# Attention and mixture of experts in one kernel: a new order of VectorE's work at the start of a round, two PSUM banks for the last attention outputs, and a second query tile scaled by GpSimd

## What is computed

```python
x = x + attention(x, mask, null_kv=cond_64)      # 16 x 256 x 256, 16 heads of 64
x = x + moe(x, cond_64)                          # 8 experts, top 2, and 2 shared ones

def attention(x):
    xn = ln(x) * g_norm
    q = l2norm(heads(xn @ Wq)) * q_scale         # per head
    k, v = split(xn @ Wkv)                       # one key and value head for all
    k = l2norm(concat(null_k, k)) * k_scale
    sim = q @ k.T * 8 + relative_bias + null_bias, causal and masked
    return ln(softmax(sim) @ concat(null_v, v) @ Wout) * g_out

def moe(x):
    w = top2(softmax((x @ wt.T + cond @ wg.T) / 2)), normalised
    y = sum(w[e] * (leaky(x @ w_gate[e]) * (x @ w_up[e])) @ w_down[e])
    return y + leaky(x @ sw_gate) * (x @ sw_up) @ sw_down
```

## Time and profile before

| | before |
|---|---|
| median of 3 runs | 1118.29 us (1117.87 to 1120.53) |
| the profiled execution | 1119.15 us, of it a span of 1117.4 us |
| PE busy | 1018.4 us (91%) |
| PEld busy | 827.5 us |
| DVE busy | 746.6 us (67%) |
| ACT busy | 534.5 us |
| POOL busy | 446.8 us |

### The profile page before, as it was taken

One profiled execution on the slowest core, in us unless ns is written; L12 is line 12 of the kernel. 1 busy time (PEld: TensorE's weight loads), 2 busy tenths in 40 slices (PEclk: granted clock), 3 DMA queues, 4 the chain that ended last, 5 costly groups with the idle time before them and its releaser, 6 DMA issues.

```text
span 1117.4 us, 22423 instructions
## 1 busy us (share of the span) xinstructions
PE 1018.4 (91%) x7244; PEld 827.5 (74%) x7244; DVE 746.6 (67%) x2515; ACT 534.5 (48%) x1579; POOL 446.8 (40%) x422
## 2 busy tenths in 40 slices
PE   2377899999989999999999999999999999999898
PEld 1266587777878787777878787787877778787777
DVE  7768858775587747765587756876487755866443
ACT  3048725663356614665256634565156543566110
POOL 2254514553435515453245424355054433355112
PEclk9588999999999999999999999999999999999999
DMA  5064411321123211311123111321113201231032
GB/s 207 19 180 156 157 39 57 106 86 41 58 77 104 67 40 58 122 62 45 60 76 115 57 58 41 105 77 67 58 58 105 83 23 43 91 105 67 20 121 106
DMA packets 40938, 89.88 MB, mean 80 GB/s; under 512 B 4128, under 2 KB 18976, under 8 KB 40304
## 3 DMA queue, kind: packets, MB, share of 16 engines
q1 hardware_dynamic: 40816, 88.29, 23.8%
HBM read 78.67 MB, written 11.70 MB: 81 GB/s over the span
## 4 chain that ended last, share of the span: by engine, by line
PE 70%; DVE 17%; issue 7%; ACT 3%; POOL 1%; SPq 1%; DMA 0%; DVEq 0%; ACTq 0%; POOLq 0%
PE psY L1479 13%; PE psO L1406 6%; PE psS L1376 6%; PE psG L65 4%; PE psG L63 4%; PE psG L64 4%; PE psT L1387 4%; PE psS L1371 3%; PE psO L1409 2%; PE psS L63 2%; PE psT L63 2%; PE psS L65 2%; PE psT L64 2%; PE psS L64 2%; PE psT L65 2%
## 5 line engine op out<-in xcount | busy, mean ns | idle before, releaser
L557 POOL TENSOR_TENSOR work<-work,rden 128x514 f32<-128x514 f32 x128 | 134.2, 1048 | 332.6 <-DVE rden L1039 332.0
L1479 PE MATMUL psY<-Wd,H 128*128 128x256 f32 x640 | 171.6, 397 | 0.0
L683 ACT ACTIVATE work<-work,low 128x257 f32<-128x257 f32 x256 | 128.3, 503 | 74.6 <-DVE low L1057 74.4
L63 PE MATMUL psG<-x1T_hi,Wgu 128*128 128x512 f32 x280 | 130.2, 465 | 7.5 <-DVE H L1157 5.6
L1479 PEld LDWEIGHTS psY<-Wd,H 128*128 128x128 f32 x640 | 111.7, 189 | 28.0 <-issue 14.4
L1057 DVE CUSTOM_DVE_ANT_0 work<-psS,bias,null_s 128x256 f32<-128x256 f32 x256 | 113.0, 478 | 23.0 <-PE psS L1376 22.5
L1147 DVE SCALAR_TENSOR_TENSOR leaky<-leaky 128x512 f32<-128x512 f32 x80 | 56.2, 703 | 98.4 <-ACT leaky L721 98.4
L65 PE MATMUL psG<-x1T_lo,Wgu 128*128 128x512 f32 x280 | 110.4, 394 | 0.0
L546 POOL TENSOR_TENSOR rq<-qss,neghalf 128x16 f32<-128x16 f32 x32 | 96.3, 3012 | 33.6 <-DVE qss L1033 33.6
L64 PE MATMUL psG<-x1T_hi,Wgu 128*128 128x512 f32 x280 | 109.4, 391 | 0.0
L675 ACT ACTIVATE qT_hi<-psO 128x256 fp32r<-128x256 f32 x128 | 49.0, 383 | 117.4 <-PE psO L1409 115.9
(11 more groups left out here) (236 smaller groups left out, 2584.7 us busy)
## 6 DMA issues: line engine op xcount, KB each, us to landing
Wgu<-wexp SPq DMA_DIRECT2D x80, 512.0 KB, 3.3
Wb<-wscr SPq DMA_DIRECT2D x64, 256.0 KB, 3.4
wexp<-Wgu SPq DMA_DIRECT2D x10, 512.0 KB, 2.9
xin<-in_x SPq DMA_DIRECT2D x8, 512.0 KB, 3.7
xres<-in_x SPq DMA_DIRECT2D x8, 512.0 KB, 4.5
out<-work SPq DMA_DIRECT2D x8, 512.0 KB, 2.9
H<-in_wgu SPq DMA_DIRECT2D x10, 256.0 KB, 4.0
bscr<-bscr SPq DMA_DIRECT2D x1, 2048.0 KB, 12.7
```

The lines of the kernel that those rows point to most:

```text
L63: te.matmul(dst, a_hi, b_hi, start=start, stop=False)
L557: pool.tensor_tensor(T1[sl][:, hs, :], T1[sl][:, hs, :], rden[sl][:, 1, hs].unsqueeze(2) .to_broadcast([P, 2, N + 1]), ALU.mult)
L683: act.activation(T1[sl][:, h, :], T1[sl][:, h, :], ACT.Exp, scale=-1.0, bias=low[sl][:, 1, h:h + 1], accum_out=den[sl][:, 1, h:h + 1])
L1479: mm = te.matmul(psY[:, t // 2, (t % 2) * D:(t % 2 + 1) * D], H[:, k % H_RING, t * P:(t + 1) * P], Wd[:, ORDER[k], :], start=(k == 0 and t ...
```

## The change

It does five things.

1. `scale_q` of tile 2 goes from VectorE to GpSimd, where it stands between the third and the fourth `rq`.
2. VectorE's `scale_q` of tile 3 moves behind the scores of step 0.
3. `null_parts` is one pair of operations on all four tiles ahead of step 0, behind all four `rq`; the pair at step 3 is gone.
4. On VectorE `sum_q(1)` goes ahead of `router_logits`, `router_shift` behind the remainder of the keys, and `hidden(1)` ahead of the second `turned_q`. On ScalarE the exponential of the router goes behind the square of tile 2.
5. `value` of steps 12 and 14 goes to psG, and 13 and 15 stay in psO. From step 12 on a value waits for the output before the last one, and for all `hidden` of the round. TensorE's wait for `pn_done`, the last read of the null column, moves ahead of `turn_x`.

```diff
-POOL_TILES = 1
+POOL_SCALED = (0, 2)
+DVE_SCALED = (1, 3)
+LAST_VALUES = 12
...
+        def value_bank(n):
+            return psG if n >= LAST_VALUES and n % 2 == 0 else psO
...
                     pool.tensor_tensor(rq[:, t, :], qss[:, t, :], neghalf[:], ALU.pow).then_inc(rq_done.sem, 1)
-                    if t < POOL_TILES:
+                    if t in POOL_SCALED:
                         scale_q(pool, r, t, qn_pool)
...
+                sum_q(r, 1)
                 if moe is not None:
                     router_logits(moe)
-                sum_q(r, 1)
-                if moe is not None:
-                    router_shift(moe)
...
                 for n in range(4):
                     turned_q(r, n)
+                    if n == 0 and moe is not None:
+                        hidden(moe, 1)
                     if n == 1 and moe is not None:
-                        hidden(moe, 1)
                         router_weights(moe)
-                scale_q(dve, r, 2, qn_done)
                 if moe is not None:
                     leak(moe, 2)
                     hidden(moe, 2)
-                scale_q(dve, r, 3, qn_done)
-                ch = vchain["null"]
-                ch.start(r)
-                null_parts(r, ch, 0)
+                null_parts(r)
...
                         scores(r, n // STEPS, n % STEPS)
+                    if n == 0:
+                        scale_q(dve, r, 3, qn_done)
...
+                need(dve, rq_done, r, TILES)
+                ch.link(dve, dve.tensor_tensor(null_s[:], kvs[:, :, 2 * DH:], rq[:], ALU.mult))
...
+                need(te, pn_done, r, GROUPS)
                 if following is not None:
                     turn_x(following)
                 need(te, o_done, r, ALL)
-                need(te, pn_done, r, GROUPS)
...
-                need(te, o_done, r, n)
+                if n < LAST_VALUES:
+                    need(te, o_done, r, n)
+                else:
+                    need(te, o_done, r, n - 1)
+                    if moe is not None:
+                        need(te, h_done, moe, BLOCKS)
+                bank = value_bank(n)
```

More of the change, by code:

```diff
@@ L316, in attention_moe @@
         qss_done = events("qss_done", TILES)
[L317 removed]
+        qn_done = events("qn_done", len(DVE_SCALED))
         qT_v = events("qT_v", 2 * TILES)
@@ L333, in attention_moe @@
         vchain = {n: Chain(events("v_" + n, k)) for n, k in
-                  (("ln1", 2), ("knorm", 3), ("null", 4), ("ln2", 2 * TILES), ("x1", TILES), ("router", 14))}
+                  (("ln1", 2), ("knorm", 3), ("null", 2), ("ln2", 2 * TILES), ("x1", TILES), ("router", 14))}
         xnT_a = events("xnT_a", 1)
@@ L352, in attention_moe @@
         rq_done = events("rq_done", TILES)
-        qn_pool = events("qn_pool", POOL_TILES)
+        qn_pool = events("qn_pool", len(POOL_SCALED))
         norm_done = events("norm_done", ALL)
@@ L625, in attention @@
                     act.activation(sq, src, ACT.Square).then_inc(sq_done.sem, 1)
+                    if t == 2 and moe is not None:
+                        softmax(moe)
                     if t == 1 and moe is not None:
@@ L674, in head_out @@
                 need(act, pv_ps, r, n + 1)
-                act.activation(qT[0][:, STEPS * (g % 2) + s, (g // 2) * N:(g // 2 + 1) * N], psO[:, 0:N],
+                act.activation(qT[0][:, STEPS * (g % 2) + s, (g // 2) * N:(g // 2 + 1) * N], value_bank(n)[:, 0:N],
                                ACT.Copy).then_inc(o_lead.sem, 1)
@@ L924, in attention @@
                 if moe is not None:
+                    router_shift(moe)
                     leak(moe, 0)
@@ L1021, in turned_q, with null_parts @@
                                   qT[0][cols].bitcast(F32), ALU.subtract).then_inc(qT_v.sem, 1)
-            def null_parts(r, ch, bb):
-                ts = slice(2 * bb, 2 * bb + 2)
-                ch.link(dve, dve.tensor_tensor(null_s[:, ts, :], kvs[:, ts, 2 * DH:], rq[:, ts, :], ALU.mult))
-                ch.link(dve, dve.tensor_tensor(null_s[:, ts, :], null_s[:, ts, :], null_bias[:].unsqueeze(1)
-                                               .to_broadcast([P, 2, HEADS]), ALU.add))
+            def null_parts(r):
+                ch = vchain["null"]
+                ch.start(r)
+                need(dve, rq_done, r, TILES)
+                ch.link(dve, dve.tensor_tensor(null_s[:], kvs[:, :, 2 * DH:], rq[:], ALU.mult))
+                ch.link(dve, dve.tensor_tensor(null_s[:], null_s[:], null_bias[:].unsqueeze(1)
+                                               .to_broadcast([P, TILES, HEADS]), ALU.add))
+                ch.end()
             def sum_q(r, t):
@@ L1083, in head_out @@
                 cols = (slice(None), STEPS * (g % 2) + s, slice((g // 2) * N, (g // 2 + 1) * N))
-                dve.tensor_tensor(qT[1][cols], psO[:, 0:N], qT[0][cols].bitcast(F32), ALU.subtract) \
+                dve.tensor_tensor(qT[1][cols], value_bank(n)[:, 0:N], qT[0][cols].bitcast(F32), ALU.subtract) \
                     .then_inc(o_done.sem, 1)
@@ L1258, in turn_q @@
                 t, half = n // 2, n % 2
-                if t < POOL_TILES:
-                    need(te, qn_pool, r, t + 1)
+                if t in POOL_SCALED:
+                    need(te, qn_pool, r, POOL_SCALED.index(t) + 1)
                 else:
-                    need(te, qn_done, r, t + 1 - POOL_TILES)
+                    need(te, qn_done, r, DVE_SCALED.index(t) + 1)
                 if n < 4:
@@ L1320, in attention @@
                     if n >= VALUE_LAG:
-                        value(r, n - VALUE_LAG)
+                        value(r, n - VALUE_LAG, moe)
                     for u in UNITS_AT.get(n, ()):
@@ L1398, in turn, with value @@
                 mm.then_inc(pt0_ps.sem, 1)
-            def value(r, n):
+            def value(r, n, moe):
                 bb = n // STEPS // 2
@@ L1403, in value @@
                 need(te, pt0_done, r, n + 1)
-                need(te, o_done, r, n)
+                if n < LAST_VALUES:
[5 more added lines that the diff above has]
+                bank = value_bank(n)
                 for i in range(2):
-                    te.matmul(psO[i * DH:(i + 1) * DH, 0:N], kvs[:, 2 * bb, DH:2 * DH], PT[n % 2][:, i, 0:N],
+                    te.matmul(bank[i * DH:(i + 1) * DH, 0:N], kvs[:, 2 * bb, DH:2 * DH], PT[n % 2][:, i, 0:N],
                               start=True, stop=False)
                 for i in range(2):
-                    mm = te.matmul(psO[i * DH:(i + 1) * DH, P:N], kvs[:, 2 * bb + 1, DH:2 * DH],
+                    mm = te.matmul(bank[i * DH:(i + 1) * DH, P:N], kvs[:, 2 * bb + 1, DH:2 * DH],
                                    PT[n % 2][:, i, N:N + P], start=False, stop=True)
```

4 lines of the change are left out of this document (removed).

## The result

The changed kernel takes 1100.93 us (median of 4 runs, 1100.15 to 1103.11), the kernel before beside it 1118.45 us (1117.87 to 1120.53): a ratio of 0.9843, 95% interval 0.9824 to 0.9862. The profiled span is 1098.7 us and was 1117.4. Forecast were 1100 us, and 18.8 us off; the spans differ by 18.7.

The account below looks back on a forecast made before the run. VectorE's queue bounds each round's start, the single bank psO its end, TensorE's own work the middle. 7 x (1.35 + 1.34) = 18.8 us off 1119.15 gives 1100.3, stated as 1100; 8-in-10 range 1094.5 to 1107.

Parts of the forecast that it names:

- The sum: Whole kernel: 7 rounds x (1.35 + 1.34) = 18.8 us off the profiled execution's 1119.15 us, giving 1100.3.
- the start: Start of each round, up to the score of step 2: shorter VectorE queue gives TensorE 1.35 us a round.
- the end: Values 13 and 15 no longer wait for outputs 12 and 14: 0.23 + 1.11 = 1.34 us a round.
- round 0: First round, without experts: loss of 1.4 against gain of 1.34 us makes 0, bounds -0.5 and +0.6.
- The collision: VectorE's leak(1) meets GpSimd's scale_q of tile 2 and ends 0.54 us after it, making VectorE 0.66 us late.
- the no-collision rival: At leak(1) the engines do not meet: 2.0 us at the round's start, 1095.8 us in all; chance 15%.
- The ScalarE wait: VectorE's wait for ScalarE's late gate copy, between scores of steps 0 and 1, some 0.74 us, goes away.
- The cover of the null pair: The null pair awaits all four rq; the fourth ends 3.1 us ahead of it, so the wait is hidden.
- the deeper collision: GpSimd's operation is held up in its turn: 0.6 to 0.8 us at the start, 1104 to 1105.5; shared chance 17%.
- GpSimd at twice VectorE's 1.22 us: Skill-page estimate for GpSimd's scale_q: leak(1) would end 0.54 us later, the total would be 1104.1 us.
- only one end pays: Rival: the other end's wait is taken over by the next semaphore; 7 x 1.35 = 9.4, 1109.8 us; chance 8%.
- Slower: Rival: fourth rq, behind GpSimd's second scale_q, ends after 449.3; at 12 us for both, 1126 us; chance 5%.

Follow-up runs that it names:

- e5: The changed kernel with scale_q of tile 2 back on VectorE in every round, behind the four turned_q; 1102.86 us, ratio to before 0.9836.
- e6: The changed kernel with hidden(1) behind two turned_q again; 1104.76 us, ratio to before 0.9850.
- e1: The kernel before with only values 12 and 14 in psG, their waits, and pn_done's wait ahead of turn_x; 1109.80 us, ratio 0.9899.
- e2: The changed kernel with all values back in psO, their old waits, and pn_done behind turn_x; 1114.19 us, ratio to before 0.9945.
- e9: The changed kernel with VectorE scaling tile 2 in round 0 alone, GpSimd in rounds 1 to 7; 1097.19 us, ratio to before 0.9796.

## Why the prediction was right

**The sum.** 7 x (1.35 + 1.34) = 18.8 us were forecast off the profiled execution and 18.7 measured. So close an agreement is partly luck: the start was set too high and the end too low, by 0.18 and 0.22 us a round, and the seven rounds and what follows them gave 18.0 us (15.65 in the six intervals, 2.3 behind the last `turn_x`). The other 0.7 us came in round 0, where the clock gave it and not the change.

**The collision** came as forecast: `leak(1)` 1.34 us, 0.54 us past GpSimd's end, in each of the seven rounds. Moving it away gave 2.9 us by the rounds, of the 4.5 by which the no-collision rival lay lower (1100.3 and 1095.8): the rival was wrong in its condition and somewhat high in its price, since the wait for H(1) shrank by 0.47 us and not by 0.6, and that of step 2 by nothing.

**The start** gives 1.17 us and not 1.35. The third `rq` stands at 429.02, and at 435.30 before, so 6.28 us bring both on one clock: `leak(2)` 439.12 + 6.28 = 445.40, as forecast; H(2) 446.18 (forecast 446.05, it waited for `up(2)`); scores of step 0 447.77 (447.57; the null pair takes 0.98 us and not 0.92); scores of step 1 452.06 (451.89), 4.29 us later where 4.32 were forecast; the score of step 2 at 453.64 (453.46). The error is made ahead of the scores of step 0 and carried on. The wait ahead of the score of step 2 is 0.58 us and not 0.2 to 0.4: VectorE is 0.18 us later than forecast, and TensorE is free 0.09 us sooner (446.78 + 6.28 = 453.06, and not 453.15). The ScalarE wait did go: `leak` at 445.18 has no bracket.

**What paid at the start** is, by more than half, the order, not GpSimd. With tile 2 on VectorE the rounds lose only 0.5 us, of the start's 1.17 (e5); the place of H(1) alone is worth 0.56 (e6). The prediction subtracted a `scale_q` of 1.13 us, put the collision (0.66) against it, and did not ask what the order alone would give.

**The end** gives 1.56 us and not 1.34: from value 12 to `turn_x` 520.72 - 514.07 = 6.65 us, where 8.21 stood before. 0.15 us of the difference is the distance of values 14, 15 and `turn_x`, 0.70 and 0.75 us and not the 0.80 that was taken from before; the rest is that of values 12 and 13, which fell by 0.30 us (1.90 to 1.60), where only the wait of 0.23 was counted. The product with Wout moved with value 15, as the argument had it: had it taken over the wait, e1 could not have given 1.46 us a round.

**Round 0** was set at 0, between -0.5 and +0.6; it gained 0.75 us in one trace of the changed kernel, outside these bounds, and 0.05 in the other. The 0.75 lies ahead of anything that was moved: the second `rq` starts 20.38 us behind `turn_x` before, 19.63 in the changed kernel's first trace and 20.27 in its second, and what differs is how long TensorE's clock stays at its lower level behind `turn_x`, some 9.6, 7.7 and 9.1 us. Behind that `rq` the step came as worked out. The scores of step 0 follow it after 10.50 us before and 11.34 in both traces after, the 0.84 us of the forecast; the start costs 1.6 us there by e2, where 1.4 was taken, the end gives 1.6 by e1; and the whole takes 73.01 us before and 73.01 and 73.08 after. VectorE's wait for `rq` is 2.96 us and was put at about 2. What the step left out is the clock: it counted waits at one speed, and TensorE works at its lower level for a third of this round, for longer or shorter from trace to trace, which moves this round by more than the bounds of 0.6 us.

**The cover of the null pair** held: 3.3 us, 3.1 forecast. **The rivals**: the deeper collision, and GpSimd at twice VectorE's 1.22 us (1104.1 us), are excluded by 1.91 us, and the wait for ScalarE is gone; "only one end pays" is excluded by e1 and e2. "Slower" was priced from 449.3 on for the fourth `rq`, which ended at 437.21 + 6.28 = 443.5.

## What to carry to other kernels

Read the two ends of a loop's body apart: where the middle belongs to one engine, gains at either end add. Before work is moved to GpSimd, look for the VectorE operation that will stand beside it, and put one that reads PSUM there. And price the first pass of a loop by itself: where the bottleneck engine pauses there, its clock can fall too, and an order that is best in the steady state may cost there, once, what it gives later (GpSimd's `scale_q`: 3.3 us on average against some 3.5 in seven rounds). Do not read the price of such a pass from one trace: the same order gave 88.1 and 91.5 us.

## What was not expected of the hardware

The collision's victim can be tiny: a 128x32 multiplication took 1.72 us beside a 1.90 us one of GpSimd. GpSimd's `rq` (a power, 128x16) takes 2.90 us, 3.28 when it begins while `leak(1)` runs, and 3.35 when it begins while a held `leak(1)` runs. In these rows it holds up nothing for the rest of its time: VectorE's `scale_q` stands inside it with 1.23 us, and the router's 128x32 multiplications, with two inputs in SBUF too, keep 0.16 to 0.20 us beside it.

TensorE's granted clock in round 0 decides more than the waits do: between e5 and e9 its idle time is 17.9 and 19.0 us, so more in the faster one, while its busy time falls from 73.60 to 69.14 us for the same work in the same order. Read from one trace of each, that would have passed for a gain of the edit.
